# A router moved to its own PSUM bank, the label diagonal on ScalarE, and state products per head

## What is computed

```python
x = x + layernorm(linear_attention(layernorm(x)))
x = x + layernorm(gated_linear_attention(layernorm(x)))
```

```python
e = softmax(x @ We)                     # 4 logits a row
mask = one_hot(argmax(e)); rw = e * mask
o = gla(q1, k1, v, gk1) + sum_e gla(q2 * rw_e, k2 * rw_e, v, gk2 * mask_e)
# gla: S_t = diag(exp(gk_t)) S_{t-1} + k_t^T v_t ; o_t = q_t S_t, 8 heads of 64
```

## Time and profile before

| | us |
|---|---|
| median of 3 runs (lowest, highest) | 3079.11 (3078.73, 3079.14) |
| the profiled execution, its own time | 3078.36 |
| its span, first to last instruction | 3076.5 |
| PE busy | 2832.1 |
| DVE busy | 2009.9 |
| ACT busy | 1676.3 |
| POOL busy | 1353.6 |

### The profile page before, as it was taken

The page is one execution under the profiler, slowest core; times in us unless marked ns, Lnnn a source line. Parts: engine busy times, 40 slices in busy tenths (PEclk is TensorE's granted clock), DMA queues, the critical chain, the costliest instruction groups (busy, mean ns, idle before and its releaser), DMA issues.

```text
span 3076.5 us, 56194 instructions
## 1 busy us (share of the span) xinstructions
PE 2832.1 (92%) x20720; PEld 1799.3 (58%) x20720; DVE 2009.9 (65%) x3750; ACT 1676.3 (54%) x3345; POOL 1353.6 (44%) x1006
## 2 busy tenths in 40 slices
PE   6999799999999999999879998999999999999997
PEld 3444466666666666666534445666666666666665
DVE  4442677777777777777544425777777777777775
ACT  4432566665565566566433425665555665565663
POOL 2873344444444444444422333444444444444443
PEclk9999899999999999999889999999999999999998
DMA  4121000000000000000021110000000000000000
GB/s 175 59 92 48 9 24 27 20 20 20 20 20 20 20 20 20 20 20 20 18 87 58 68 41 18 21 20 20 20 20 20 20 20 20 20 20 20 20 20 11
DMA packets 48376, 97.49 MB, mean 32 GB/s; under 512 B 5376, under 2 KB 5376, under 8 KB 47680
## 3 DMA queue, kind: packets, MB, share of 16 engines
q1 hardware_dynamic: 37008, 68.44, 6.6%
q10 hardware_dynamic: 9792, 17.83, 1.6%
q0 software_dynamic: 1520, 10.50, 0.9%
HBM read 63.19 MB, written 33.55 MB: 31 GB/s over the span
## 4 chain that ended last, share of the span: by engine, by line
PE 84%; DVE 9%; ACT 4%; issue 2%; POOL 1%; DMA 0%; POOLq 0%; SPq 0%; ACTq 0%; DVEq 0%
PE psum L304 13%; PE psum L306 12%; PE psum L305 12%; PE psum L451 12%; PE psum L551 5%; DVE lscore L1135 5%; PE psum L426 4%; PE psum L440 4%; PE psum L460 4%; PE psum L416 4%; PE psum L354 2%; PE psum L313 2%; ACT ogT L737 2%; PE psum L433 2%; PE psum L353 2%
## 5 line engine op out<-in xcount | busy, mean ns | idle before, releaser
L984 POOL TENSOR_TENSOR region<-region,kfac 128x512 f32<-128x512 f32 x64 | 66.7, 1042 | 780.6 <-DVE kfac L1198 780.6
L451 PE MATMUL psum<-region 128*128 128x128 f32 x2560 | 366.5, 313 | 10.8 <-POOL region L966 10.8
L451 PEld LDWEIGHTS psum<-region 128*128 128x128 f32 x2560 | 358.8, 229 | 11.1 <-issue 11.1
L966 POOL TENSOR_TENSOR region<-region,mb 128x512 f32<-128x512 f32 x256 | 322.5, 1287 | 73.5 <-ACT region L624 73.0
L999 POOL TENSOR_TENSOR region<-region,decay 64x1280 f32<-64x1280 f32 x128 | 298.1, 2329 | 117.7 <-DVE decay L1214 112.4
L304 PE MATMUL psum<-wb,region 128*128 128x512 f16 x768 | 292.1, 380 | 3.0 <-DVE mb L1163 3.0
L305 PE MATMUL psum<-wb,region 128*128 128x512 f16 x768 | 292.3, 381 | 0.0
L306 PE MATMUL psum<-wb,region 128*128 128x512 f16 x768 | 292.2, 380 | 0.0
L958 POOL TENSOR_TENSOR region<-region 128x1024 f32<-128x1024 f32 x64 | 146.6, 2291 | 287.5 <-DVE region L1313 229.9
L979 POOL TENSOR_SCALAR region<-region,m 128x512 f32<-128x512 f32 x256 | 172.2, 692 | 222.9 <-DVE hm L1147 147.9
L1313 DVE SCALAR_TENSOR_TENSOR region<-psum,region 128x512 f16<-128x512 f32 x64 | 44.3, 692 | 261.1 <-ACT region L798 261.1
(11 more groups left out here) (232 smaller groups left out, 7623.1 us busy)
## 6 DMA issues: line engine op xcount, KB each, us to landing
region<-x_in SPq DMA_DIRECT2D x128, 256.0 KB, 2.7
q_cols<-region ACTq DMA_DIRECT2D x64, 256.0 KB, 2.3
region<-q_cols SPq DMA_DIRECT2D x64, 256.0 KB, 2.9
out_rows<-region SPq DMA_DIRECT2D x60, 256.0 KB, 2.0
region<-wb_in POOLq DMA_DIRECT2D x1, 3072.0 KB, 12.1
region<-wqkv_in SPq DMA_DIRECT2D x4, 512.0 KB, 6.6
region<-wqkv_in POOLq DMA_DIRECT2D x2, 1024.0 KB, 5.7
region<-wproj_in POOLq DMA_DIRECT2D x2, 1024.0 KB, 7.5
```

Of the source, the lines that this page charges most:

```text
L451: last = mm(bank[7][:, pr * P:(pr + 1) * P], q, state[:, pr, path, :], start=(pr == 0 and path == 0), stop=False, skip_group_check=True)
L966: last = nc.gpsimd.tensor_tensor(qm[:, e, :, :], q2T, mb[:, e, :].unsqueeze(1).to_broadcast([P, PAIRS, P]), ALU.mult)
```

## The change

- The router logits go to columns 128 to 131 of bank 0 (a new PE function `route`, between `low_rank` and `project_v`, with a semaphore of its own, `route_pe`). `low_pe` is given before them.
- ACT no longer copies the logits to SBUF (`logit_s` and `low0_ok` are gone). DVE's `front_router` reads them in PSUM: `lmax`; then `lscore`, as `(logit == lmax) * score`; then `ldiff`, unscaled (ACT scales by 1/64 inside its exponential).
- The diagonal `lab_i` is made by ACT (`front_label`, behind `front_v`), no longer by DVE.
- DVE's `m4` and `hm` move behind `back_carry`, as `front_onehot`.
- `label_bc` on PE waits for `ldiff_ok` (its bank still holds the logits until then).
- `state_products`: the dense products are 8 matmuls of 64 by 64, one per head, in place of 4 of 128 by 128, one per pair of heads of which only the diagonal blocks were used. `back_carry1` reads them as 256 columns side by side.

```diff
-        logit_s = cut(4)
...
@@ PE
             def low_rank(n):
...
                     for g in range(KT):
-                        mm3(bank[7][:, part * P:(part + 1) * P], lambda x: wl[:, x, g, part * P:(part + 1) * P],
+                        last = mm3(bank[7][:, part * P:(part + 1) * P], lambda x: wl[:, x, g, part * P:(part + 1) * P],
                             lambda x: xnT[:, x, g, :], g == 0, g == KT - 1)
+                last.then_inc(S("low_pe"), 1)
+
+            def route(n):
+                pe.wait_ge(S("am1_ok"), prev(n))
                 for g in range(KT):
-                    last = mm3(bank[7][:, 2 * P:2 * P + NEXP], lambda x: xnT[:, x, g, :], lambda x: wl[:, x, g, 2 * P:],
+                    last = mm3(bank[0][:, P:P + NEXP], lambda x: xnT[:, x, g, :], lambda x: wl[:, x, g, 2 * P:],
                                g == 0, g == KT - 1)
-                last.then_inc(S("low_pe"), 1)
+                last.then_inc(S("route_pe"), 1)
 
             def label_bc(n):
                 pe.wait_ge(S("labi_ok"), cur(n))
-                pe.wait_ge(S("am1_ok"), prev(n))
+                pe.wait_ge(S("ldiff_ok"), cur(n))
...
             def gates(n):
                 pe.wait_ge(S("low_ok"), cur(n))
-                pe.wait_ge(S("low0_ok"), cur(n))
...
                 for pr in range(PAIRS):
-                    mm(bank[1][:, pr * P:(pr + 1) * P], k1g[:, pr * P:(pr + 1) * P], v[:, p, pr * P:(pr + 1) * P], start=True, stop=True)
+                    for odd in range(2):
+                        h = 2 * pr + odd
+                        mm(psum[odd * D2:odd * D2 + D2, 1, pr * D2:(pr + 1) * D2],
+                           k1g[:, h * D2:(h + 1) * D2], v[:, p, h * D2:(h + 1) * D2], start=True, stop=True)
...
                     low_rank(n)
+                    route(n)
                     project_v(n)
@@ ACT
-                ac(logit_s, bank[7][:, 2 * P:2 * P + NEXP], ACT.Copy, scale=1.0 / W_SCALE).then_inc(S("low0_ok"), 1)
...
+            def front_label(n):
+                act.wait_ge(S("lab_ok"), n + 1)
+                act.wait_ge(S("rx_pe"), prev(n))
+                ac(lab_i[:, :], ident16[:, :], ACT.Copy, scale=lab[:, :]).then_inc(S("labi_ok"), 1)
+
             def front_router(n):
-                act.wait_ge(S("ldiff_ok"), n + 1)
-                ac(lexp[:, :], ldiff[:, :], ACT.Exp, accum_out=lsum[:, :]).then_inc(S("lexp_ok"), 1)
+                act.wait_ge(S("ldiff_ok"), cur(n))
+                ac(lexp[:, :], ldiff[:, :], ACT.Exp, scale=1.0 / W_SCALE, accum_out=lsum[:, :]).then_inc(S("lexp_ok"), 1)
...
                     front_v(n, p)
+                    front_label(n)
                     front_gates(n, 0)
@@ DVE
-                    last = ve.tensor_tensor(carry[h, :, 0, :], bank[1][h, :].rearrange("p (a b) -> p a b", a=PAIRS)[:, :, h],
+                    last = ve.tensor_tensor(carry[h, :, 0, :], bank[1][h, 0:PAIRS * D2].rearrange("p (a b) -> p a b", a=PAIRS),
                                             state[h, :, 0, h], ALU.add)
...
             def front_router(n):
-                dve.wait_ge(S("low0_ok"), cur(n))
-                ve.reduce_max(lmax[:, :], logit_s, X).then_inc(S("lmax_ok"), 1)
+                dve.wait_ge(S("route_pe"), cur(n))
+                logits = bank[0][:, P:P + NEXP]
+                ve.reduce_max(lmax[:, :], logits, X).then_inc(S("lmax_ok"), 1)
                 dve.wait_ge(S("lmax_ok"), n + 1)
-                ve.tensor_scalar(ldiff[:, :], logit_s, lmax[:, :], None, ALU.subtract).then_inc(S("ldiff_ok"), 1)
-                dve.wait_ge(S("ldiff_ok"), n + 1)
-
-                ve.scalar_tensor_tensor(lscore[:, :], ldiff[:, :], 0.0, score, ALU.is_equal, ALU.mult).then_inc(S("lscore_ok"), 1)
+                ve.scalar_tensor_tensor(lscore[:, :], logits, lmax[:, :], score, ALU.is_equal, ALU.mult).then_inc(S("lscore_ok"), 1)
+                ve.tensor_scalar(ldiff[:, :], logits, lmax[:, :], None, ALU.subtract).then_inc(S("ldiff_ok"), 1)
 
             def front_label(n):
                 dve.wait_ge(S("lscore_ok"), n + 1)
                 ve.reduce_max(lab[:, :], lscore[:, :], X).then_inc(S("lab_ok"), 1)
+
+            def front_onehot(n):
                 dve.wait_ge(S("lab_ok"), n + 1)
-                dve.wait_ge(S("rx_pe"), prev(n))
-                ve.tensor_scalar(lab_i[:, :], ident, lab[:, :], None, ALU.mult).then_inc(S("labi_ok"), 1)
                 dve.wait_ge(S("vm_ok"), prev(n))
                 ve.tensor_scalar(m4[:, :], score, lab[:, :], None, ALU.is_equal).then_inc(S("m4_ok"), 1)
...
                     back_carry(m)
                 if front:
+                    front_onehot(n)
                     front_masks(n)
```

More of the change, by code:

```diff
@@ L209, in sandwich_kernel @@
             "scalar": ["xT4_full", "kh_ok", "q_read", "xh_ok",
-                       "xnT_ok", "low1_ok", "low0_ok", "lexp_ok", "abs_ok", "ex_ok", "ln_ok", "sig_ok",
+                       "xnT_ok", "low1_ok", "labi_ok", "lexp_ok", "abs_ok", "ex_ok", "ln_ok", "sig_ok",
                        "v_ok", "ke_ok", "e1_ok", "e2_ok", "exs_ok", "q1T_ok", "k1T_ok", "q2T_ok", "k2T_ok",
                        "osq_ok", "ogT_ok", "z_ok", "xc_ok", "xnh_ok", "x1m_ok"],
-            "vector": ["xn8_ok", "xf_ok", "kl_ok", "low_ok", "x1_ok", "xn_ok", "am1_ok", "am2_ok", "carry1_ok", "carry_ok", "labi_ok",
+            "vector": ["xn8_ok", "xf_ok", "kl_ok", "low_ok", "x1_ok", "xn_ok", "am1_ok", "am2_ok", "carry1_ok", "carry_ok", "ldiff_ok",
                        "same_ok", "mb_ok", "ls_ok", "lsl_ok", "sil_ok", "kd_ok", "k1g_ok", "q1g_ok", "q2g_ok",
@@ L216, in sandwich_kernel @@
             "tensor": ["xT4_pe", "q_pe", "k_pe", "moment_pe", "y_pe", "tr_pe", "a_pe", "t_pe", "u_pe", "low_pe",
-                       "inter_pe", "rx_pe", "g_pe", "o_pe", "k2_pe", "q1_pe", "cum1_pe", "cum_pe", "sum_pe",
+                       "inter_pe", "rx_pe", "route_pe", "g_pe", "o_pe", "k2_pe", "q1_pe", "cum1_pe", "cum_pe", "sum_pe",
                        "den_pe", "og_pe", "wo_pe", "v_pe"],
```

## The result

The changed kernel takes 2854.16 us (median of 4 runs, 2852.98 to 2854.88) against 3078.94: a ratio of 0.927, 95% interval 0.9254 to 0.9286. The forecast was 2874, in a range from 2842 to 2952. It is faster, by 225 us where 205 were forecast. The profiled execution spans 2853.0 us.

The account below looks back on a forecast made before the run. PE's own order bounds the second pass, with one stall at `gates` waiting for DVE. Stall -129.0, clock falls -75.9 and products 0 give -204.9 us, from 3078.4 to 2873.5, said as 2874; range 2842 to 2952.

Parts of the forecast that it names:

- The stall: PE's wait before `gates` for DVE's `low_ok`, 2.08 us a step, was to go: -129.0 us over 62 steps.
- the 0.31 us of `ldiff`: DVE's `ldiff` in the router, read as taking 0.31 us by itself, a usual length beside POOL's work.
- The clock: Falls of PE's granted clock after the idle at `gates` were to vanish: -75.9 us.
- rival (a): Clock falls stay, tied to the narrow matmuls around PE's idle and not to the idle; 2950 us median, chance 0.08.
- Rival (b): A remnant of the wait at `gates`, 0.35 us a step, stays; 2896 us, up to 2940 with some falls; chance 0.10.
- my margin of 0.15 us: At `gates`, DVE's result was to let PE restart at 1036.6, PE arriving at 1036.75: 0.15 us to spare.
- the 1.38 us: Time from the start of DVE's `front_low` to PE's restart at `gates`, taken over from the kernel before.
- The products: PE's 16 dense state-product instructions in place of 8: 0.86 us against 0.89 a step, taken as no change, 0.
- -0.42 as the low end: Dense state products on PE if cost goes with moving columns: 0.47 us, -0.42 a step, -27 us in all.
- The cover of the diagonal and of the masks: ACT's label diagonal hidden by `gates` and `project_k2`, 0.6 us to spare; one-hot masks hidden before `project_k`; no cost.
- Rival (e): Slower: `lscore` still stands behind POOL, through `score` in SBUF, or comparing is slow; 3098 us, chance 0.03.

Follow-up runs that it names:

- sum_in_halves: The kernel before, with POOL's sum of the two score tiles made in two instructions of 512 columns; 2936.59 us, ratio 0.9537.
- score_from_sbuf: The changed kernel, with `ldiff` computed first from PSUM, then `lscore` from `ldiff` and `score`, both in SBUF; 2859.73 us.
- score_first: The kernel before, only DVE's order changed: `lscore` from the SBUF logits ahead of `front_low`, `ldiff` behind it; 2874.41 us, ratio 0.9335.
- heads_only: The kernel before, with only the dense state products made per head in place of per pair; 3112.61 us, ratio 1.0109.

## Why the prediction was right, and where it was off

The stall: the -129.0 us held. That `lscore` stood behind POOL's sum is shown: 2.26 us beside the sum, 1.18 us when the sum is cut in two (sum_in_halves), 0.16 us with POOL idle. That an input in PSUM spares it the standing is shown for the last product (0.22 us, where it is 0.61 from SBUF), not for the sum. And the prediction took this for what removes the stall, which it is only in small part. score_from_sbuf, with both tensors in SBUF again, loses 5.6 us, and score_first, with nothing in PSUM, keeps 204. What removed the stall is that `lscore` no longer comes behind the start of the sum, which it had missed by 0.10 us in every step. The prediction's own times said so: logits read from 1034.42 and `lmax` of 0.16 us put `lscore` at about 1034.6, ahead of the sum's start at 1035.06, where it could not stand behind the sum from whichever memory it read. So the size was right, and part of the reason was luck: the edit that brought the input into PSUM also brought the instruction forward.

The prediction also took the 0.31 us of `ldiff` for its own length. It is 0.23 with POOL idle; the rest is standing behind the last product, 0.08 us in the step shown and up to 0.16 in others, and heads_only has up to 0.45 us of it. How much of the gain comes from `ldiff` no longer reading SBUF, and how much from its place and from the logits read without ACT's copy, is not separated by these runs; the order alone is enough.

The clock: all 75.9 us came back, and rival (a) is out. Rival (b), a remnant: my margin of 0.15 us was 0.42. Of the difference, 0.06 is the hand-over from `low_ok` to PE, which I had counted in the 1.38 us. The rest is that `front_low` starts earlier against PE, 1.74 us ahead of `gates` (1002.56 and 1004.30) and not 1.55. I had taken `lscore` and `ldiff` at up to 0.31 us each; they take 0.22 and 0.21, and overlap. `front_low` then starts 0.04 us behind ACT's third operation (1002.26 + 0.26 = 1002.52), so ACT, not the router, may be what it waits for. That PSUM operands are no dearer here held: `lmax` is 0.16 us from either, and `lscore` in the form `(logit == lmax) * score` takes 0.22 us from PSUM and 0.22 us from SBUF with POOL idle (the first step of a pass in score_first). The Trainium skill (VectorE: DVE Perf Modes, The TRN2 errata) has a larger fixed term for PSUM sources; these rows speak against it.

The products: this is the term that was mis-sized. I took 0 and kept -0.42 as the low end; it is -0.28 a step, -18 us, 0.038 us for each of 16. They lie between a cost by moving columns (0.029) and one by stationary columns (0.054). 2874 - 18 = 2856, and 2854 was measured. By the Trainium skill (TensorE: Matmul & The Clock Gate, LDWEIGHTS) they were an estimated 0.85 us; the 0.61 measured is less.

The cover of the diagonal and of the masks held. The diagonal took ACT 0.40 us, not 0.26, and ended at 1005.52, 0.48 us ahead of `label_bc`.

Rival (e) is out: `lscore` still reads `score` in SBUF and still compares, and takes 0.22 us beside the last product. Beside the sum it was not tried.

## What to carry to other kernels

When a tiny DVE operation takes microseconds, look whether a POOL instruction ends within a few hundredths of a microsecond of it, and at the operation before it: it may have waited too, and lost the turn for it. Then find a step in which POOL is idle, for its length alone. Two things helped here: another place in DVE's order, ahead of the long POOL instruction (204 us by itself), and an input in PSUM (5.6 us here, once the place was right). Try the order first, it costs nothing. A miss of 0.10 us cost 2.08 us a step. And a part that shortens PE's work is worth nothing while PE waits for something that does not move, so price parts in the order in which the waits fall, with the clock's loss behind each idle added.

## What was not expected of the hardware

A DVE operation with one SBUF input (`ldiff`, 128x4; the diagonal, 128x128) also stands behind a POOL instruction: 0.68 and 0.93 us where it takes 0.23 and 0.29 with none beside it. The Trainium skill (SBUF — State Buffer, Who interferes with whom) says that copies, casts and scalar operations can enter modes that use the shared pair. My working had left it out; the trace agrees in that both ended with POOL's instruction (0.02 and 0.09 us behind it), though no row shows the mode. Between two POOL instructions in a row, the one DVE operation that already stands has its turn (score_from_sbuf), and the next one, issued 0.04 us later, finds the second POOL instruction running and stands for all of it (heads_only). A kernel can get 34 us slower from less work on PE alone, through the clock: with an idle of 2.21 in place of 1.91 us a step, 48 in place of 42 of 62 intervals have a fall, and 20 in place of 4 a long one.
